# Joined exact attention body, and out-degree norms in the build's tail with convolution 1 group by group

## The reference

```python
# layer 0: two graph convolutions, with a batch norm and a sigmoid between them
out_deg = segment_sum(ones, src);  in_deg = segment_sum(ones, dst)
out_norm = rsqrt(clip(out_deg, 1.0));  in_norm = rsqrt(clip(in_deg, 1.0))
agg = segment_sum((x * out_norm[:, None])[src], dst)
conv = agg * in_norm[:, None] + bias
# layer 2: graph attention, twice, each with a graph norm behind it
e = leaky((h @ a_src)[src] + (h @ a_dst)[dst], 0.2)
ex = exp(e - segment_max(e, dst)[dst]);  alpha = ex / segment_sum(ex, dst)[dst]
out = segment_sum(h[src] * alpha[:, None], dst) + b
```

## Time and profile before

| | us |
|---|---|
| median of three runs | 868.24 |
| the profiled execution, its own time | 876.73 |
| span of the profile | 875.0 |
| TensorE busy | 750.4 (86%) |
| DVE busy | 626.6 (72%) |
| ACT busy | 481.2 (55%) |
| granted TensorE clock, mean | 0.926 |

### The profile page before, as it was taken

The page is one execution under the profiler, slowest core; times in us unless marked ns, Lnnn a source line. Parts: engine busy times, 40 slices in busy tenths (PEclk is TensorE's granted clock), DMA queues, the critical chain, the costliest instruction groups (busy, mean ns, idle before and its releaser), DMA issues. The chain is left out here.

```text
span 875.0 us, 21046 instructions
## 1 busy us (share of the span) xinstructions
PE 750.4 (86%) x8192; PEld 677.5 (77%) x8192; DVE 626.6 (72%) x1691; ACT 481.2 (55%) x916; POOL 4.3 (0%) x14
## 2 busy tenths in 40 slices
PE   7888888868988999999997399988656999887898
PEld 6655556548987998999997298887655898776797
DVE  7899999985355454433444789998787999885632
ACT  2798889861004222212235578887576988773600
POOL 1000000000000000000000000000000000000000
PEclk9799999998997999999997589999956999996999
DMA  4000000007960000000002100000000699839401
GB/s 135 11 12 12 12 3 1 1 5 262 413 282 1 2 1 2 2 1 1 13 24 81 33 16 4 16 17 1 1 14 20 141 176 200 169 80 233 106 22 36
DMA packets 98739, 56.06 MB, mean 64 GB/s; under 512 B 91160, under 2 KB 93130, under 8 KB 98504
## 3 DMA queue, kind: packets, MB, share of 16 engines
q1 hardware_dynamic: 98292, 53.78, 22.3%
q10 hardware_dynamic: 340, 0.84, 0.3%
HBM read 9.16 MB, written 24.97 MB: 39 GB/s over the span
## 5 line engine op out<-in xcount | busy, mean ns | idle before, releaser
L614 PE MATMUL banks<-y_sb,adjacency 128*128 128x192 f16 (+1 forms) x1875 | 166.4, 249 | 8.5 <-DVE y_sb L651 7.8
L614 PEld LDWEIGHTS banks<-y_sb,adjacency 128*128 128x128 f16 x1875 | 162.0, 99 | 9.5 <-DVE y_sb L651 7.9
L457 PE MATMUL counts<-hot_code,hot_row 128*128 128x100 f16 (+3 forms) x1568 | 122.3, 217 | 23.2 <-DVE hot_code L351 17.6
L457 PEld LDWEIGHTS counts<-hot_code,hot_row 128*128 128x128 f16 x1568 | 90.7, 99 | 66.0 <-DVE hot_code L351 41.3
L1752 PE MATMUL banks<-loose,y_sb 128*128 128x194 f16 x540 | 101.1, 251 | 0.0
L1751 PE MATMUL banks<-x_sb,gat_masks 128*128 128x194 f16 x420 | 79.6, 251 | 20.7 <-DVE gat_masks L1676 6.8
L351 DVE TENSOR_TENSOR hot_code<-codes_iota,unpacked 128x600 f16<-128x600 f16 x196 | 96.7, 552 | 0.0
L560 ACT ACTIVATE adjacency<-counts 128x800 f16<-128x800 f32 x98 | 81.7, 834 | 21.5 <-PE counts L457 21.4
L1751 PE MATMUL banks<-x_sb,y_sb 128*128 128x194 f16 x400 | 75.1, 250 | 13.6 <-DVE h_sb L1676 9.9
L1724 ACT ACTIVATE gat_masks<-y_sb,node_scalars 128x640 bf16<-128x640 f32 x84 | 68.0, 825 | 26.5 <-PE banks L1752 19.3
L1751 PE MATMUL banks<-x_sb,h_sb 128*128 128x194 f16 x430 | 75.8, 247 | 0.8
(11 more groups left out here) (246 smaller groups left out, 1358.4 us busy)
## 6 DMA issues: line engine op xcount, KB each, us to landing
kept_adj<-adjacency SPq DMA_DIRECT2D x5, 4000.0 KB, 31.8
y_sb<-a_dst_rows SPq DMA_DIRECT2D x10, 320.0 KB, 3.4
window_keys<-edge_keys SPq DMA_DIRECT2D x188, 5.0 KB
residual<-h_sb SPq DMA_DIRECT2D x5, 240.0 KB, 2.0
kept_x<-x_sb SPq DMA_DIRECT2D x1, 1200.0 KB, 4.6
loose<-residual SPq DMA_DIRECT2D x5, 240.0 KB, 4.6
x_sb<-kept_x SPq DMA_DIRECT2D x5, 240.0 KB, 4.8
x_sb<-in_x SPq DMA_DIRECT2D x4, 240.0 KB
```

Source lines behind the costliest of these rows:

```text
L457: last = nc.tensor.matmul(counts[:, 2 * (p % HELD) + i, start:end], hot_row[:, q % 2, b * QUAD + w, :], hot_codes(q % 2, b)[:, w, start - ...
L614: return nc.tensor.matmul(k.ps[:, j % G, 0:cols], k.ADJ[:, i, j * P:(j + 1) * P], y[:, i, 0:cols], start=i == 0, stop=i == NT - 1)
```

## The change

- The clip, the product with the variance, the square root and the reciprocal of the out-degree norms move from the head of `convolutions` into the tail of `build_adjacency`: DVE clips and multiplies before the total, ACT loads its table behind its last store and takes the root, and DVE takes the reciprocal before it loads the flag. The general build, which is not run, repeats them for its own degrees. `k.clipped` and `k.roots` are allocated earlier.
- In convolution 1 DVE no longer centres all groups first. It centres group 0, and then per group multiplies, centres the next one and writes the low part.
- The exact path has one body: a loop over eight chunks of four tiles, which start three tiles apart (`STRIDE` = 3) and so overlap by one tile. The second copy is gone, and so is the unrolled first round of the probabilities: two is added to `used` beforehand, and all waits count from there.

```diff
...
@@ -374,12 +375,20 @@
 
+        def products_of_norms(done):
+            chain(dve.tensor_scalar(k.clipped[:, 0, :], k.out_deg[:, :], 1.0, None, ALU.max))
+            dve.tensor_tensor(k.clipped[:, 1, :], k.clipped[:, 0, :], k.var0[:, :], ALU.mult).then_inc(done, 1)
+
         dve.wait_ge(degree_ready, 1)
...
         dve.tensor_scalar(k.out_deg[:, :], k.out_deg[:, :], 1 / UNIT, None, ALU.mult).then_inc(out_deg_ready, 1)
+        dve.wait_ge(out_deg_ready, 1)
+        products_of_norms(clipped)
         dve.wait_ge(total_ready, 1)
...
         dve.tensor_scalar(missed, total[:, :], float(E), None, ALU.is_lt).then_inc(flag_ready, 1)
+        dve.wait_ge(rooted, 1)
+        chain(dve.reciprocal(k.roots[:, :, :], k.roots[:, :, :]))
         dve.wait_ge(flag_ready, 1)
@@ -410,6 +419,9 @@
             chain(dve.tensor_scalar(k.out_deg[:, :], k.out_deg[:, :], 1 / UNIT, None, ALU.mult))
+            products_of_norms(g_clipped)
+            dve.wait_ge(g_rooted, 1)
+            chain(dve.reciprocal(k.roots[:, :, :], k.roots[:, :, :]))
 
@@ -559,6 +571,9 @@
                                  counts_of(2 * (p % HELD), 2), ACT.Copy, scale=UNIT).then_inc(stored, 1)
+        act.preload_act_table(ACT.Sqrt)
+        act.wait_ge(clipped, 1)
+        nc.scalar.activation(k.roots[:, :, :], k.clipped[:, :, :], ACT.Sqrt).then_inc(rooted, 1)
         act.wait_ge(stored, PAIRS)
...
@@ -786,22 +803,22 @@
 
-        chain(dve.tensor_scalar(k.clipped[:, 0, :], k.out_deg[:, :], 1.0, None, ALU.max))
-        dve.tensor_tensor(k.clipped[:, 1, :], k.clipped[:, 0, :], k.var0[:, :], ALU.mult).then_inc(s.clipped, 1)
-        for g in range(NG):
+        def centre(g):
             dve.tensor_tensor(tiles(k.H, g), tiles(k.X, g), across(group(k.mean0, g)), ALU.subtract).then_inc(s.centred, 1)
 
-        chain(dve.memset(k.Y[:, :, ONE:YC], 1 / UNIT))
-        dve.wait_ge(s.root, 1)
-        chain(dve.reciprocal(k.roots[:, :, :], k.roots[:, :, :]))
-        dve.wait_ge(s.centred, NG)
-        for g in range(NG):
+        def value(g):
+            dve.wait_ge(s.centred, g + 1)
             nc.vector.scalar_tensor_tensor(out=tiles(k.H, g), in0=tiles(k.H, g), scalar=0.0,
...
                                            op0=ALU.max, op1=ALU.mult).then_inc(s.value, 1)
-            if g >= 1:
-                dve_low(nc, k, dve, g - 1, s.high, s.y_ready, k.Y)
-        dve_low(nc, k, dve, NG - 1, s.high, s.y_ready, k.Y)
+
+        centre(0)
+        chain(dve.memset(k.Y[:, :, ONE:YC], 1 / UNIT))
+        for g in range(NG):
+            value(g)
+            if g + 1 < NG:
+                centre(g + 1)
+            dve_low(nc, k, dve, g, s.high, s.y_ready, k.Y)
 
@@ -891,8 +908,6 @@
     def _(act):
-        act.wait_ge(s.clipped, 1)
-        nc.scalar.activation(k.roots[:, :, :], k.clipped[:, :, :], ACT.Sqrt).then_inc(s.root, 1)
         for g in range(NG):
@@ -1370,8 +1385,8 @@
 NC = NT // CHUNK
-REST = NT % CHUNK
 SHIFT_STEPS, ROUND = 5, 6
+CHUNKS, STRIDE = 8, 3
 ACC, TURN, ROWS_U, ROWS_V, OUT, OTHER_OUT = 0, 1, 2, 3, 6, 0
@@ -1428,10 +1443,10 @@
         def cols(ch, n):
-            return slice(ch * CW, ch * CW + n * P) if isinstance(ch, int) else bass.ds(ch * CW, n * P)
+            return bass.ds(ch * (STRIDE * P), n * P)
 
         def nodes(ch, n):
-            return slice(ch * CHUNK, ch * CHUNK + n) if isinstance(ch, int) else bass.ds(ch * CHUNK, n)
+            return bass.ds(ch * STRIDE, n)
 
@@ -1476,24 +1491,19 @@
 
-            def probability(ch, i, e, n, wait=True):
+            def probability(ch, i, e, n):
                 dve.wait_ge(s.small, ch * NT + (i + 1))
-                if wait:
-
-                    dve.wait_ge(s.used, ch * NT + (i - 1))
+                dve.wait_ge(s.used, ch * NT + (i + 1))
                 nc.vector.scalar_tensor_tensor(out=prob[:, e % 2, 0:n * P], in0=k.ps[:, EXPS[e % len(EXPS)], 0:n * P], scalar=BIG,
...
                 larger(ch, 0, 0, n)
-                for e in range(ROUND):
-                    larger(ch, e + 1, (e + 1) % len(EXPS), n)
-                    probability(ch, e, e, n, e >= 2)
-                with dve.Fori(0, NT // ROUND - 1) as r:
+                with dve.Fori(0, NT // ROUND) as r:
                     for e in range(ROUND):
-                        larger(ch, r * ROUND + (e + 1 + ROUND), (e + 1) % len(EXPS), n)
-                        probability(ch, r * ROUND + (e + ROUND), e, n)
+                        larger(ch, r * ROUND + (e + 1), (e + 1) % len(EXPS), n)
+                        probability(ch, r * ROUND + e, e, n)
                 probability(ch, NT - 1, 0, n)
@@ -1517,6 +1527,7 @@
             dve.sem_inc(s.larger, 1)
+            dve.sem_inc(s.used, 2)
 
@@ -1524,11 +1535,10 @@
 
-            with dve.Fori(0, NC) as ch:
+            with dve.Fori(0, CHUNKS) as ch:
                 chain.loop(ch, SHIFT_STEPS + 1)
                 chunk(ch, CHUNK)
-            chain.end(NC)
-            chunk(NC, REST)
+            chain.end(CHUNKS)
             for n in range(NC + 1):
...
@@ -1561,12 +1570,11 @@
 
-                act.wait_ge(s.used, (ch + 1) * NT)
+                act.wait_ge(s.used, (ch + 1) * NT + 2)
                 nc.scalar.activation(out_sb[0:C + 1, 0:n * P], k.ps[0:C + 1, OUT, 0:n * P], ACT.Copy).then_inc(s.out_copied, 1)
 
-            with act.Fori(0, NC) as ch:
+            with act.Fori(0, CHUNKS) as ch:
                 exponentials(ch, CHUNK)
-            exponentials(NC, REST)
 
...
@@ -2077,6 +2084,8 @@
         k.out_deg, k.mean0, k.var0 = (sb(n, [P, NT], F32) for n in ("out_deg", "mean0", "var0"))
+        k.clipped, k.roots = sb("clipped", [P, 2, NT], F32), sb("roots", [P, 2, NT], F32)
+        k.out_norm = k.roots[:, 0, :]
         with ExitStack() as c2:
...
```

More of the change, by code:

```diff
@@ L201, in build_adjacency @@
         sem("degree_ready"), sem("out_deg_ready"), sem("total_ready"), sem("flag_ready"))
+    clipped, rooted, g_clipped, g_rooted = sem("clipped"), sem("rooted"), sem("g_clipped"), sem("g_rooted")
     dve_chain, pool_chain = sem("dve_chain1"), sem("pool_chain1")
@@ L571, in _ @@
             act.wait_ge(g_stored, NW + 1)
+            act.wait_ge(g_clipped, 1)
+            nc.scalar.activation(k.roots[:, :, :], k.clipped[:, :, :], ACT.Sqrt).then_inc(g_rooted, 1)
 PARTS = 2
@@ L747, in convolutions @@
 def convolutions(nc, k, d, c, block):
-    s = semaphores(nc, k, "c1", "chain vectors columns centred clipped root value high "
+    s = semaphores(nc, k, "c1", "chain vectors columns centred value high "
                    "y_ready summed emptied in_clipped in_root factor h_ready tiles_turned measured var_h dev_h affine gated back")
@@ L1545, in diagonals @@
                                        of[:, 0:n].unsqueeze(2).to_broadcast([P, n, P]), ALU.mult).then_inc(s.diag_ready, 1)
-            with pool.Fori(0, NC) as ch:
+            with pool.Fori(0, CHUNKS) as ch:
                 diagonals(ch, CHUNK)
-            diagonals(NC, REST)
         def exact_scalar(act):
@@ L1603, in chunk @@
                 turn_output(ch, n)
-            with pe.Fori(0, NC) as ch:
+            with pe.Fori(0, CHUNKS) as ch:
                 chunk(ch, CHUNK)
-            chunk(NC, REST)
-            pe.wait_ge(s.h_written, NC + 1)
+            pe.wait_ge(s.h_written, CHUNKS)
             turn_tiles(nc, k, pe, t.tiles_turned, 0, NT)
@@ L1795, in _ @@
                 if last:
-                    sp.wait_ge(s.h_written, NC + 1)
+                    sp.wait_ge(s.h_written, CHUNKS)
                     load_back(k, d, sp)
@@ L2097, in network @@
         k.T2 = y32[:, NT * YC // 2:NT * YC // 2 + 2 * G * C].rearrange("p (a t f) -> p a t f", a=2, f=C)
-        k.clipped, k.roots = sb("clipped", [P, 2, NT], F32), sb("roots", [P, 2, NT], F32)
-        k.out_norm = k.roots[:, 0, :]
         scalars = sb("node_scalars", [P, 11, NT], F32)
```

## The result

The changed kernel takes 868.77 us (median of 22 runs, 864.96 to 872.38). The kernel before, run beside it on the same chip, takes 874.0 (22 runs, 868.05 to 878.0). The ratio is 0.9952, with a 95% interval of 0.9933 to 0.997: faster by 0.48%, which is 4.2 us of 874.0; the two medians stand 5.2 apart. The forecast had the direction and about the size of the change right (-4.2) and the time wrong: 864.0 was forecast, with 866.7 as the upper end of the range. The profiled execution took 870.68 us, its span 868.9 (before 876.73 and 875.0), at a mean granted clock of 0.933 (0.926).

A forecast was written before the change was run, and what follows sets the result against it. TensorE, busy 86% of the span, was taken as the bound, so its idle waits count. Convolution 1's head net of the build's tail, -2.5, and the attention stall, -1.7, gave -4.2 from 868.24: 864.0 us, range 862.2 to 866.7.

The forecast's parts named there:

- block opens after the last store, longer by: Build's tail: DVE, already level with the last to arrive, reaches its branch later; +0.6 us, bounds +0.1 and +0.8.
- block opening to first product: Head of convolution 1: the first group is ready 2.8 us after the block opens instead of 5.9; -3.1 us.
- clock at the restart: Convolution 1: TensorE restarts cold again and its clock rises after the same 5.0 us; change taken as 0.
- TensorE's start behind the first mask, layer 1: First attention: DVE's code stall behind the branch goes, so TensorE starts at 500.95 instead of 502.73; -1.7 us.
- TensorE's stall, layer 2: Second attention: if TensorE's branch stall goes, 0.5 of 1.3 us is kept; nothing was taken for it.
- one of the bounds of the forecast: Clock rise after a restart, 3.6 to 6.5 us in the attention layers: 0.7 us cheaper or 0.75 dearer; 0 taken.
- the last of the sum: Runs shown, median 868.24, were taken to lie 8.5 below the profiled execution for lack of a profiler; 4.2 subtracted there.
- The rival in which only the head counts: Convolution 1's head gains 2.5 us, the attention's code stall stays because code alignment decides; 865.7 us, chance 0.26.
- The rival of new code stalls: ACT's or TensorE's branch in both layers stalls newly, up to 3.9 us each; 872.5 us, chance 0.06.
- the clock stays up: Convolution 1: the shorter wait keeps TensorE's clock from falling, saving 2.5 us more; 861.5 us, chance 0.05.
- length decides: Attention branches: DVE's jump shrinks from about 205 instructions to about 100, below ACT's unstalled 130, so its stall goes.
- half-long blocks: Code fetch: if DVE's blocks are half of 256 instructions, the two-block rule explains its stall and passes the shorter jump.

The follow-up runs named there:

- the pair with fills: Filling matmuls nobody reads, at the second attention's end and the last layer's head, added to the kernel before (870.56 us) and to the changed kernel (863.84 us).
- the last layer's fills: Changed kernel plus 20 and 25 filling matmuls at the end of the second attention and 56 instead of 28 at the last layer's head: 863.84 us.
- all additions: Changed kernel plus filling matmuls for convolution 1 and the last layer, and DVE's reciprocal in the build's tail not awaited: 862.24 us, ratio 0.989.
- The shifted code: Kernel before with met waits added ahead of convolution 1's work, 60 instructions on DVE and 128 on TensorE: 882.42 us, ratio 1.0116.
- both shifted kernels: Met waits added to the kernel before (60 instructions on DVE, 128 on TensorE; 882.42 us) and to the changed kernel (45 and 128; 876.68 us, one run).

## Why the prediction was wrong in the time and right in the change

The terms, forecast and measured (us, profiled executions of before and after):

| term | forecast | measured |
|---|---|---|
| block opens after the last store, longer by | +0.6 | +0.52 |
| block opening to first product | -3.1 | -3.08 |
| clock at the restart: up again after | 5.0 | 5.1 |
| TensorE's start behind the first mask, layer 1 | -1.7 | -1.68 |
| its clock, up after 6.5 us, now 5.2, and the rest of the layer | 0 (bounds -0.7 to +0.75) | -0.65 |
| TensorE's stall, layer 2 | 0 | -0.65, but see below |
| build and layer 0 outside the change | 0 | -0.55 |
| sum | -4.2 | -6.1 |

The last two rows: 0.30 us of the 0.55 is a last store that ends earlier and 0.25 the way from first product to first mask, which varied from 296.2 to 298.4 between kernels whose work is the same there. The 0.65 behind the second mask holds the last layer too, whose clock was down for 20.5 us before and 17.1 after. In the pair with fills nothing is left of it, so "I take nothing" stands, though TensorE's start comes 1.2 earlier (3.85 to 2.62 behind the mask). The stretch between the two masks is 2.3 shorter in every kernel with one exact body, 1.7 for the start and the rest for the clock that rises 1.4 us sooner after it: one of the bounds of the forecast came true. The ratio of the runs gives 4.2, within an interval of 2.6 to 5.9 (0.003 and 0.0067 of 874.0), and the medians 5.2; the steps of the change itself, 2.56 + 2.3 = 4.9, lie between. That 4.2 was forecast and 4.2 came out to the tenth is luck: the steps are 0.7 larger, nearly all of it the clock of the first attention.

That the clock is up 5.1 us after the restart in convolution 1, forecast 5.0, is luck too. In the eleven kernels without fills there it took from 2.7 to 5.9 us, and in three with the same head as the changed kernel 3.3, 4.5 and 4.8.

**The step that failed is the last of the sum.** "The median of the runs shown, 868.24, is 8.5 below because they carry no profiler." No run shows such a cost. Before's 876.73 lies among its own 22 runs, 868.05 to 878.0, and the profiles of the changed kernel and of the experiments are themselves among the timed runs: 863.96 in 862.58 to 865.47 with the last layer's fills, 861.82 in 861.18 to 862.89 with all additions. Every run on record has a span and a granted clock beside its time, so none is known to carry no profiler, and what it costs was not measured; the sentence ahead of the forecast by which the profiled execution "is longer than the runs without the profiler" rests on the same guess. What the runs show in its place is the spread of the kernel itself, for the most part the 6.9 us of the last layer. The three runs shown happened to be of the lower group, the profile of the upper (no trace of a lower run of before was kept; its time and the fills say so); 22 runs have their median at 874.0. Subtracting 4.2 from the lower group's value set the range around a base 5.8 below the median, so its upper end of 866.7 was missed by 2.1. Had the change been laid on the profile's own 876.73, the 872.5 would have been too high by 3.7: a single profile does not say how often each group comes. But the profile held the warning, and no rows of it stood in the forecast: 20.5 us at 1.2 GHz in the last layer, with TensorE's records busy for 18.2 of them. A stretch whose clock can be up or down at the same code had to widen the range, or be looked for when three runs agree within 0.8 us and the profile stands 8.5 away.

**The other steps.** That DVE was level with the last to arrive, so that all of its delay counts, holds: TensorE drains at 194.0, DVE at 194.5, and without the wait for the reciprocal 0.48 comes back. No group behind the first was late; the `low` parts come every 1.9 us (forecast 1.95). The rival in which only the head counts (0.26) is refuted by the kernel with only the exact body changed. The rival of new code stalls (0.06) did not occur. That the clock stays up (0.05) did not either, but when made to, it gave 2.3 us. Two readings of the forecast were off without moving its sum: the clock of the second attention rose at 669.7, 3.9 us after the first matmul at 665.78 and not 3.6, which makes the cheaper end of the bounds 0.5 and not 0.7; and of the 37 products put at the low clock, six ran behind the rise (31 take 5.16 us, 0.166 each, so 4.2 and not 3.8 for a group).

**Why the stall was there.** The forecast had "length decides" and left half-long blocks as a possibility. The shifted code shows that length and place decide together. Counted in the program, with DVE's blocks taken as 128 instructions, its branch stood at place 79 of a block in the first layer and 29 in the second, and jumps 205: to 284 and to 234, one beyond two blocks (256) and one not. Shifted by 60, it stands at 11 and 89 and lands at 216 and 294, and the stall is in the other layer, as measured. The jump of 102 ends within two blocks from any place. The Trainium skill (Runtime: NRT & Kernel Launch, Instruction fetch mechanics) gives that rule with blocks of 256 instructions, by which none of DVE's jumps could stall; by the 0.29 MB in 35 packets of queue 14 against 1.11 MB in 68 of queue 8, DVE's are half as long, if queue 14 is DVE's (the profile names no engine for the instruction queues), and with that the rule agrees with these four places, and with the short jump wherever it stood. TensorE's stall is not settled: the jump of about 210 stalled in one layer of two in five kernels that kept it, and a shift of 128 moved it; the jump of 152 never did in the eight that have it, also shifted by 128. With blocks as long as queue 8's packets the rule would let both through.

## What to carry to other kernels

Before a change is subtracted from a median, check that the profile and the median are of the same kind of run: a profile that stands 1% away from runs that agree among themselves can be another behaviour of the kernel, to be looked for in the clock of some stretch, before it is put down to measuring. Code that is jumped over is not free when the jump is about as long as what an engine holds ready, and shortening it was worth about as much here (2.3 us) as reordering work that runs (2.3 of 2.56). Ahead of a stretch that depends on TensorE's clock, matmuls into an unused bank, placed in waits, gave 2.3 us in one place and took most of a spread of 7 us away in another.

## What the runs showed of the hardware

- Back-to-back fp32 products held TensorE's records busy for 15 us (14.90 of 14.90, from 798.1 to 813.0 before) without the clock coming up. The f16 pass of convolution 1 had it up 2.7 to 5.9 us after its start in the eleven kernels that let it fall, and that of the first attention 3.4 to 6.6 (5.1 to 5.3 in six of the eight with the short jump). In other executions it rose within the fp32 stretch of the last layer. Why the same code keeps its clock in one execution and not in the next was not settled.
- Waits on TensorE that are already met and stand as instructions of their own start 0.11 us apart (127 recorded in 13.9 us, in both shifted kernels), two waits to an instruction.
- A branch that stalled cost DVE 2.0 to 2.8 us (2.86, 3.17 and 3.63 behind the mask instead of 0.86) and TensorE 2.9 to 3.7 (3283 to 4103 ns instead of 312 to 381).
